# Second layer's attention with four maps of 32 columns a group and denominators summed apart, and attention's causal masks added to the scores by TensorE in three layers

## What is computed

```
xn = layernorm(x);  x = x + attention(xn) + feed_forward(xn)
```

```
y = causal_attn(q1, k1, v) - lam * causal_attn(q2, k2, v)      # v is 32 wide, two maps a head
p = softmax(where(mask, q k^T * scale, -inf));  causal_attn = p v
```

## Time and profile before

| | |
|---|---|
| median of 3 runs | 4427.25 us (4421.09 to 4436.3) |
| the profiled execution | 4430.29 us, span 4428.6 us |
| mean granted TensorE clock | 0.907 |
| PE busy | 3624.9 us (82%) |
| PE weight loads | 2176.7 us (49%) |
| DVE busy | 2584.7 us (58%) |
| ACT busy | 1880.7 us (42%) |
| POOL busy | 834.9 us (19%) |

### The profile page before, as it was taken

One profiled execution on the slowest core, in us unless ns is written; L12 is line 12 of the kernel. 1 busy time (PEld: TensorE's weight loads), 2 busy tenths in 40 slices (PEclk: granted clock), 3 DMA queues, 4 the chain that ended last, 5 costly groups with the idle time before them and its releaser, 6 DMA issues. The chain is left out here.

```text
span 4428.6 us, 62889 instructions
## 1 busy us (share of the span) xinstructions
PE 3624.9 (82%) x23244; PEld 2176.7 (49%) x23244; DVE 2584.7 (58%) x5480; ACT 1880.7 (42%) x2902; POOL 834.9 (19%) x1018
## 2 busy tenths in 40 slices
PE   5876786778768889888893889887988988898897
PEld 3424333334256373553732666656653653663672
DVE  5746666647555464554556555455665664765764
ACT  2262361452656556464662434343126125216216
POOL 3012111120122030120300323232311220220220
PEclk8887897888889999899996989998999999999999
DMA  5312403214140000000002000002000000000000
GB/s 189 120 38 68 130 29 111 86 59 121 41 154 1 5 25 6 24 1 29 1 6 79 5 24 29 5 24 79 1 1 30 1 1 29 1 1 30 1 1 11
DMA packets 147088, 177.11 MB, mean 40 GB/s; under 512 B 16384, under 2 KB 123392, under 8 KB 146688
## 3 DMA queue, kind: packets, MB, share of 16 engines
q1 hardware_dynamic: 139008, 153.81, 11.0%
q0 software_dynamic: 6144, 16.79, 1.2%
q10 hardware_dynamic: 1632, 2.49, 0.2%
HBM read 126.40 MB, written 51.38 MB: 40 GB/s over the span
## 5 line engine op out<-in xcount | busy, mean ns | idle before, releaser
L741 DVE TENSOR_REDUCE arena<-ps 128x2 f32<-128x1024 f32 (+3 forms) x768 | 698.8, 952 | 167.7 <-PE ps L709 94.8
L937 ACT ACTIVATE arena<-ps 128x1024 f32<-128x1024 f32 (+3 forms) x768 | 577.4, 812 | 236.9 <-PE ps L846 187.1
L1020 DVE TENSOR_TENSOR arena<-arena,tri 128x256 f32<-128x256 f32 x512 | 209.0, 422 | 329.1 <-ACT arena L937 317.4
L846 PE MATMUL ps<-arena 64*128 64x512 f16 (+3 forms) x1536 | 260.0, 353 | 139.4 <-ACT arena L937 89.4
L937 ACT ACTIVATE attention<-ps 128x1024 f32<-128x1024 f32 (+3 forms) x384 | 287.9, 809 | 187.3 <-PE ps L846 187.3
L863 PE MATMUL ps<-arena 128*17 128x512 f32 (+3 forms) x3072 | 349.4, 529 | 14.3 <-DVE arena L1020 12.2
L2591 ACT ACTIVATE arena<-ps 128x256 f32<-128x256 f32 x192 | 63.6, 381 | 620.2 <-PE ps L2533 575.0
L846 PEld LDWEIGHTS ps<-arena 64*128 64x128 f16 x1536 | 71.3, 94 | 496.2 <-ACT arena L937 387.5
L863 PE MATMUL ps<-attention,live 128*33 128x512 f32 (+3 forms) x1536 | 290.6, 502 | 0.0
L709 PE MATMUL ps<-arena 64*128 64x512 f16 (+3 forms) x1536 | 237.3, 335 | 50.4 <-DVE arena L741 31.6
L1190 PE MATMUL ps<-gated_parts,weight_parts 128*128 128x256 f32 x1536 | 219.0, 300 | 30.0 <-DVE operands L1291 30.0
(11 more groups left out here) (330 smaller groups left out, 7054.0 us busy)
## 6 DMA issues: line engine op xcount, KB each, us to landing
arena<-w_experts SPq DMA_DIRECT2D x128, 256.0 KB
acc<-sums SPq DMA_DIRECT2D x16, 1024.0 KB, 5.7
x_next<-sums SPq DMA_DIRECT2D x16, 1024.0 KB, 8.3
arena<-slots_x SPq DMA_DIRECT2D x32, 512.0 KB, 4.6
slots_y<-arena SPq DMA_DIRECT2D x32, 512.0 KB, 4.3
sums<-acc SPq DMA_DIRECT2D x24, 512.0 KB, 2.9
making<-basis SPq DMA_DIRECT2D x16, 768.0 KB, 6.3
slots_x<-arena SPq DMA_DIRECT2D x1, 4096.0 KB, 29.4
```

What stands on the lines that cost most here:

```text
L741: dve.reduce_max(a.mp[:, 2 * j:2 * j + 2, qt, c], out[:, :, 0:w], AX.X).then_inc(self.pair_out, 1)
L846: last = pe.matmul(m.ps[:, 4 + 2 * (v % 2) + odd, q0:CH], a.k[half, pair, kt * P:(kt + 1) * P], a.q[half, pair, c * CH + q0:(c + 1) * CH], ...
L937: act.activation(a.p[:, v % ring, :, q0:CH], m.ps[:, b:b + 2, q0:CH], ACT.Exp, scale=HD ** -0.5).then_inc(exped, 1)
L1020: dve.tensor_tensor(diag, diag, keep, ALU.min).then_inc(masked, 1)
```

## The change

1. Masks (all twelve calls). The tile `above` (bf16, -1e30 above the diagonal, 0 elsewhere) takes the place of `tri`. After a diagonal pair's two score matmuls, PE adds `above` to the first 128 columns of each of the two banks, by a bf16 matmul with the identity as weights on all 128 rows. DVE's masks and PE's wait for `masked` are gone.
2. Layer 1 runs as groups of 4 maps of 32 columns: 4 groups, two pairs a unit, one unit a block. The values matmuls leave out the column of ones.
3. Denominators (layer 1 only, `apart`): the exp of kt = 0 goes into a tile `total` (6 slots) instead of the ring; the probabilities of the other kt are added to it in float32 as 128x2x(width) tensors, by DVE for kt 1 to 3 in chunk 1 and by POOL for all the rest. Per unit (c, g), PE sums `total` over the partitions with columns of ones (`sum_total`, four float32 maps, into the bank that `keep_sums` has emptied), DVE adds that to `totals` (`keep_total`). Four transposes and `invert` a chunk give the reciprocals, once for all heads; `give` then only scales and subtracts. Finishing pieces start four blocks later in layer 1.
4. The exp of a ring slot also waits for the addition that reads the slot.

The diff, cut to its core:

```diff
3646.00:3651.60 5.60DIFF3646.00:3651.60 5.60
```

More of the change, by code:

```diff
@@ L767, in sync_rows, with attention @@
         self.sync_end(sp)
-def attention(nc, m, a, maps, width, wout, out_scale, batch, store=None, routed=None):
+def attention(nc, m, a, maps, width, wout, out_scale, batch, store=None, routed=None, apart=False):
     groups, pairs = NM // maps, maps // 2
@@ L805, in first_query, with added_by @@
         return max(kt * P, c * CH) - c * CH
[L807 to L813, removed]
-        ahead = NextNormalisation(m, next_sems, root_by_vector=True) if store is not None else None
+    def added_by(n):
+        c, g, kt = units[n]
+        if kt == 0:
+            return None
+        return "vector" if c == 1 and kt < TC else "pool"
@@ new lines, in additions, with total, probabilities @@
+    def additions(engine, n):
+        return pairs * sum(added_by(i) == engine for i in range(n))
+    in_ring = [v for v in range(pairs * n_units) if not apart or units[v // pairs][2] > 0]
+    ring_place = {v: i for i, v in enumerate(in_ring)}
+    totalling = {last_of[unit] + lag + 2: unit for unit in range(NC * groups)} if apart else {}
+    sums_turning = groups * TC + lag + 3
+    def total(unit, j):
+        return a.total[:, (pairs * unit + j) % a.total.shape[1]]
+    def probabilities(v):
+        n, j = divmod(v, pairs)
+        c, g, kt = units[n]
+        if apart and kt == 0:
+            return total(c * groups + g, j)
+        return a.p[:, ring_place[v] % ring]
@@ L942, in _ @@
             step = Steps(dve, steps)
-            keep = m.tri[:, :].unsqueeze(1).broadcast_to([P, 2, P])
             def add(t):
@@ new lines, in add_total @@
+            def add_total(n):
+                c, g, kt = units[n]
+                for j in range(pairs):
+                    dve.wait_ge(exped, pairs * n + j + 1)
+                    if kt == 1:
+                        dve.wait_ge(summed, n)
+                    else:
+                        dve.wait_ge(vector_added, additions("vector", n - 1) + j + 1)
+                    t = total(c * groups + g, j)
+                    dve.tensor_tensor(t, t, probabilities(pairs * n + j), ALU.add).then_inc(vector_added, 1)
@@ new lines, in keep_total @@
+            def keep_total(unit):
+                dve.wait_ge(totalled, unit + 1)
+                if unit >= 1:
+                    dve.wait_ge(totals_kept, unit)
+                if unit % groups == 0:
+                    if unit:
+                        dve.wait_ge(totals_turned, unit // groups)
+                    dve.tensor_copy(a.totals[:, :], m.ps[:, unit % 2, :]).then_inc(totals_kept, 1)
+                else:
+                    dve.tensor_tensor(a.totals[:, :], a.totals[:, :], m.ps[:, unit % 2, :],
+                                      ALU.add).then_inc(totals_kept, 1)
@@ L1013, in _ @@
                     combine(block - COMBINED)
-                for v in range(2 * block, 2 * block + 2) if block < n_blocks else ():
-                    n = v // pairs
-                    q0 = first_query(n)
-                    if on_diagonal(n):
-                        dve.wait_ge(exped, v + 1)
-                        diag = a.p[:, v % ring, :, q0:q0 + P]
-                        dve.tensor_tensor(diag, diag, keep, ALU.min).then_inc(masked, 1)
                 if ahead is not None:
@@ L1055, in attention_scratch @@
     a.yt = ar.take(2, D)
-    a.z = ar.take(2, D // 2)
+    a.z = ar.take(D)
     a.p = ar.take(ring, 2, CH)
+    a.total = ar.take(totals, 2, CH)
+    a.totals = ar.take(CH)
+    a.column = ar.take(CH // 4)
 def attention_memory(m, ar, heads, vd, groups, ring):
```

146 lines of the change are left out of this document (117 added, 29 removed).

## The result

The changed kernel took 4508.52 us (median of 4 runs, 4503.9 to 4517.86) against 4424.17 us of the kernel before in the same comparison: a ratio of 1.0188, interval 1.0171 to 1.0205, so 83 us slower. Forecast were 96 more and 4523 us. Size and sign came out; the split between the layers did not.

A forecast was written before the change was run, and what follows sets the result against it. TensorE was taken to pace layer 1, ScalarE to be nearest the bound in layers 0 and 3. Adding 80 us there and 16 in layer 1 to 4430.3 gave 4526, by the median 4523 us; range 4425 to 4600.

The forecast's parts named there:

- the split between the layers: Whole kernel: masks in layers 0 and 3 were to add 80 us, layer 1 another 16 us.
- Masks on TensorE, price of a block: Diagonal blocks: a masked pair costs 0.22 us before values, 0.35 before another score; 0.57 a block, 0.12 per change of shape.
- What hides it: Layers 0 and 3: free TensorE time hides only 0.24 us per chunk 1 group (+2.0 left); chunk 0 groups +1.2.
- 0.5 for chunk 0's last group: Layers 0 and 3: masks add only 0.5 us there, as VectorE's late normalisation chain gets 8 masks (3.4 us) back.
- Layer 1, additions: 20.4 us a group: Layer 1, chunk 1: POOL's contended work of 14.6 us plus a 5.8 us gap sets each group's period.
- The loop: Layer 1, chunk 1: POOL's last addition, sum_total, keep_total, VectorE's kt 2 and 3, then POOL's kt 4; 5.8 us between POOL's work.
- Chunk 0: "it just fits", 36 us: Layer 1, chunk 0: POOL's 7.7 us a group fits beside TensorE's 7.8; layer 3's 32 us plus masks 4.
- The end: 3.4 + 11.8, 139 in all: Layer 1 after POOL's fourth end at 124: 3.4 us through reciprocals, 11.8 for last four tiles; call 139 against 136 before.
- Much slower: Rival, chance 0.15: POOL and VectorE hold each other up whenever they overlap; loop 24 us a group, 4567 to 4600 us.
- Faster: Rival, chance 0.16: layer 1's additions keep up, chunk 1 groups take 15.5 us, masks stay at their lower bound; 4375 us.
- level: Rival, chance 0.09: layer 1's additions keep up, but masks cost the forecast price; 4438 us, or 4435 by the median.
- the signs named: Profile signs: layers 0 and 3 loops +10, diagonal units 7.6 us, mask 0.32 behind score, layer 1 values 44, POOL busy 85 to 95.

## Why the prediction was right, and where wrong

*Masks on TensorE, price of a block.* Right: 0.54 for 0.57, with 0.11 at a change of shape. Over no masks at all they cost 10.4 a call.

*What hides it.* A group in chunk 1 lost 1.44, not 2.0, and the four of a call 4.9, not 8: the free time was 0.7, not the 0.24 that busy time left. In chunk 0, +1.3 for 1.2: right.

*"0.5 for chunk 0's last group."* This is the step that failed. I gave VectorE back the 3.4 us of the group's own masks and let TensorE's masks use them up. The group fell by 3.4 to 5.1 us: all the masks ahead of it had made the normalisation's chain late, and the chain held the transposes. Counting the waits for masks (12.2 us over 8 batches) had missed that, since the wait that the masks caused stood under another name, L374. With it, layers 0 and 3 lose 33 us by the spans (30 to 47 by the ratios), not 80.

*Layer 1, additions: 20.4 us a group.* Right in sum (19.3 to 22.1), but by two errors that cancel, so by luck: less time lost to contention in POOL's work, a longer gap. The loop has two links, the sum of totals and the ring of probabilities; opening the first gave 15 us.

*Chunk 0: "it just fits", 36 us.* Wrong: 39.8. POOL's rate did fit. What didn't was VectorE's chain of small steps beside POOL, which I had costed at nothing: 0.17 us steps became 0.65 to 1.7, each held until POOL's addition beside it was done. Without POOL's additions chunk 0 takes 33.9.

*The end: 3.4 + 11.8, 139 in all.* Wrong: 146.8. POOL's last addition ended 126.3 into the call (forecast 124), but from there it took 20.5 us, not 15.2: 5.1 instead of 3.4 up to the reciprocals, then 15.4 instead of 11.8. I had taken the pace of layer 3's last tiles; here `give` is three VectorE steps in a row for each tile, and the granted clock over these tiles was 0.70, where layer 3's was 1.00. So layer 1 loses 45 us, not 16.

*Much slower as a rival* had the right mechanism, VectorE and POOL in each other's way, at the wrong place: it is dear in chunk 0's small steps and mild in chunk 1's large additions, which the loop keeps mostly apart. Faster and level are out: POOL's period never came near 15 us.

*Of the signs named:* the loops of layers 0 and 3 grew by 3.6 to 6.7 and not by 10, a group's diagonal units took 7.1 and not 7.6, POOL was busy 76 in the loop and 83 in the call (85 to 95 forecast); the mask 0.32 behind the score and the 44 us of values came out.

## To carry to other kernels

Before moving work off an engine or onto one, look at what stands in order behind it, not only at who waits for the work itself: much of what VectorE's masks cost was a late normalisation, and a large part of what POOL's additions cost was the same chain, held up. In this kernel additions with both inputs in SBUF were better left on VectorE alone than shared with POOL, even with VectorE at 86% of the loop. And the small matmul that had to be slipped in between others was cheapest on the rows of its neighbours.

## What the runs showed of the hardware

- VectorE and POOL in each other's way, in numbers: a VectorE float32 addition of 1024 elements takes 1219 ns alone and 2591 in the mean beside POOL's; POOL's takes 2.33 us alone, 3.2 when it starts beside one of VectorE's, 2942 ns in the mean with both at it. VectorE steps of 8 elements take 0.17 us, and as much as 1.7 when they begin beside an addition of POOL: in layer 1 all forty of these ended 0.02 to 0.03 us behind it.
- Between 64-row scores, full-array masks and 32-column values, going from one shape to the next cost 0.1 to 0.11 us at the granted clock 1.00; where mask and score had the same 64 rows, 0.01.
- The same four last tiles took 15.3 us at a granted clock of 0.83 and 19.1 at 0.50, with the same instructions on TensorE and VectorE.
